# Another order of the pieces in layer 0's rounds, and RWKV mixing and scan as one section with the key-value products in PSUM

## The reference

```
layer 0 (16 heads of 128 columns, D = 256, FF = 1024)
  twice:  h = layer_norm(x);  q = h wq + bq;  k = ctx wk + bk;  v = ctx wv + bv
          one more key and value per head (bias_k, bias_v)
          x = x + softmax(q k / sqrt(128)) v wo + bo
  then:   x = x + gelu(layer_norm(x) w_fc1 + b_fc1) w_fc2 + b_fc2

layer 1 (RWKV, 32 heads of S1 = 8 columns)
  xn = layer_norm(x); sx = xn shifted by one row - xn
  five mixed inputs w, k, v, r, g: xn + sx * (maa + tanh((xn + sx maa_x) w1) w2)
  kT, vT, rT = mixed inputs times Wk, Wv, Wr;  gT = silu(mixed g times Wg)
  wT = exp(-exp(time_decay + tanh(mixed w decay_w1) decay_w2))
  per head: y[t] = r[t] (state[t] + faaaa k[t] v[t]);  state[t+1] = w[t] state[t] + k[t] v[t]
  group norm over each head's 8 columns, times gT, times Wo, added to x
  then channel mixing (a second small section)
layers 2 and 3: two small cross-attentions and a last norm; not touched
```

## Time and profile before

| | |
|---|---|
| median of 3 runs | 1342.48 us (1341.75 to 1343.86) |
| the profiled execution, its own time | 1343.32 us |
| its span, first to last instruction | 1341.6 us |
| what lies around the span | 1.7 us |
| granted TensorE clock, mean | 0.95 |
| layer 0 | 0 to 750 us |
| layer norm of layer 1 | 750 to 761 us |
| mixing | 761 to 832 us |
| scan with all behind it | 832 to 956 us |
| channel mixing | 956 to 986 us |
| layers 2 and 3 | 986 to 1341.6 us |
| busy over the span | PE 88%, PEld 68%, DVE 65%, POOL 48%, ACT 47% |

### The profile page before, as it was taken

The page is one execution under the profiler, slowest core; times in us unless marked ns, Lnnn a source line. Parts: engine busy times, 40 slices in busy tenths (PEclk is TensorE's granted clock), DMA queues, the critical chain, the costliest instruction groups (busy, mean ns, idle before and its releaser), DMA issues. The chain is left out here.

```text
span 1341.6 us, 20628 instructions
## 1 busy us (share of the span) xinstructions
PE 1184.0 (88%) x7388; PEld 907.9 (68%) x7388; DVE 871.7 (65%) x2094; ACT 636.0 (47%) x1425; POOL 647.6 (48%) x673
## 2 busy tenths in 40 slices
PE   6999999999999999999989688766658998899994
PEld 4887888888888788888877533422445775666664
DVE  5776666766667666676665343997555565766666
ACT  3655565555655555655542123002123673477770
POOL 3565665656556565565751031442001672277760
PEclk9999999999999999999999789797799899999997
DMA  5110211101111011210102000000030000000000
GB/s 199 64 48 17 64 64 63 49 17 63 64 64 48 19 61 64 63 48 25 55 17 78 16 1 0 1 0 0 0 88 0 1 2 1 1 1 2 1 2 32
DMA packets 35111, 47.06 MB, mean 35 GB/s; under 512 B 3865, under 2 KB 22082, under 8 KB 35010
## 3 DMA queue, kind: packets, MB, share of 16 engines
q1 hardware_dynamic: 34640, 44.83, 10.4%
q10 hardware_dynamic: 370, 0.91, 0.2%
HBM read 44.69 MB, written 1.05 MB: 34 GB/s over the span
## 5 line engine op out<-in xcount | busy, mean ns | idle before, releaser
L444 POOL TENSOR_TENSOR a_prob<-a_prob,a_inv_total 128x512 f32<-128x512 f32 x128 | 144.1, 1126 | 217.6 <-DVE a_inv_total L732 217.6
L1593 POOL TENSOR_TENSOR l_scores<-l_scores,l_neg_max 128x512 f32<-128x512 f32 x144 | 147.8, 1040 | 99.1 <-DVE l_neg_max L1583 98.8
L1583 DVE CUSTOM_DVE_ANT_0 l_scores<-psum,mask 128x256 f32<-128x256 f32 x384 | 139.8, 421 | 69.6 <-PE psum L1536 69.6
L637 ACT ACTIVATE a_prob<-psum,a_neg_max 128x257 f32<-128x257 f32 x256 | 118.9, 472 | 93.0 <-DVE a_neg_max L729 92.0
L1614 ACT ACTIVATE l_prob_T<-psum 128x512 f32<-128x512 f32 x192 | 108.8, 590 | 34.3 <-PE psum L1550 34.3
L1550 PE MATMUL psum<-ident,l_scores 128*128 128x128 f32 x768 | 116.4, 290 | 7.0 <-POOL l_scores L1593 3.9
L1550 PEld LDWEIGHTS psum<-ident,l_scores 128*128 128x128 f32 x768 | 85.1, 145 | 41.1 <-issue 18.8
L736 DVE TENSOR_TENSOR a_probT_lo<-psum,a_probT_hi 128x512 fp32r<-128x512 f32 x128 | 87.9, 687 | 23.0 <-ACT a_probT_hi L641 22.5
L729 DVE TENSOR_REDUCE a_neg_max<-psum 128x2 f32<-128x514 f32 x128 | 87.3, 682 | 1.3 <-PE psum L486 1.3
L566 PE MATMUL psum<-ident,a_prob 128*128 128x128 f32 x512 | 77.6, 274 | 6.8 <-POOL a_prob_bias L447 6.8
L641 ACT ACTIVATE a_probT_hi<-psum 128x512 fp32r<-128x512 f32 x128 | 76.6, 599 | 9.3 <-PE psum L566 9.3
(11 more groups left out here) (322 smaller groups left out, 3325.4 us busy)
## 6 DMA issues: line engine op xcount, KB each, us to landing
wk_raw<-in_L_xattn_wk SPq DMA_DIRECT2D x16, 512.0 KB, 6.4
wq_raw<-in_L_xattn_wq SPq DMA_DIRECT2D x16, 512.0 KB, 5.7
wv_raw<-in_L_xattn_wv SPq DMA_DIRECT2D x16, 512.0 KB, 3.7
wo_raw<-in_L_xattn_wo SPq DMA_DIRECT2D x16, 512.0 KB, 4.1
ctx_rows<-in_ctx SPq DMA_DIRECT2D x3, 512.0 KB, 4.2
x_rows<-in_x SPq DMA_DIRECT2D x2, 512.0 KB, 9.5
mask<-in_mask_Bx1xSxS_ff SPq DMA_DIRECT2D x1, 1024.0 KB, 8.0
out_dram<-fin_y SPq DMA_DIRECT2D x4, 256.0 KB, 2.1
```

What stands on the lines that cost most here:

```text
L444: pool.tensor_tensor(prob[:, m % 4, :, 0:S], prob[:, m % 4, :, 0:S], rtot[:, m % 4, :].unsqueeze(2).to_broadcast([P, 2, S]), ALU.mult)
L637: act.activation(prob[:, m % 4, q, 0:S + 1], s_bank(g)[:, q, 0:S + 1], ACT.Exp, bias=negm[:, m % 4, q:q + 1], accum_out=tot[:, m % 4, q:q ...
L1583: e = dve.tensor_tensor_reduce(sc[:, i % SC, q, :], s_bank(i)[:, q * S:(q + 1) * S], masks[:, b * NM + q % NM, :], 1.0, BIG, ALU.add, ALU. ...
L1593: pool.tensor_tensor(sc[:, i % SC, :, :], sc[:, i % SC, :, :], m[:, i % SC, :].unsqueeze(2).to_broadcast([P, 2, S]), ALU.subtract).then_in ...
```

## The change

Layer 0: the last pieces of a round change places, S7 before A1, Q3 behind T6, K3 last; the statistics X and the normalising Y become four pieces of one row block each, behind T1 to T4, X in rounds with i % 4 = 0 and Y in those with i % 4 = 1 (POOL's rstd_of moves to the end of the former); L0 and L1 stand behind S0 and S2. A score piece waits for its own head's Q and K alone, and key_columns follows K2 in place of K3.

Layer 1: the two blocks become one, without the barrier. The constants are built at its start, vT's parts during the last mixing, the mixing's products use banks 4 to 7 from pv on, and the first two spreads are issued between mg, pr and pg. The products k v are written back to the PSUM banks that held the spread values; the first state is copied there for each chunk, and the recurrence reads PSUM. POOL's scan_z products wait for one chunk alone. faaaa times k moves to ACT and its product with r to POOL, behind POOL's first scan_z; the product of scan_ru with vT moves from DVE to POOL; the gate (g_T) comes in DVE's order behind the second step. Several tiles share memory. The arithmetic is the same.

```diff
@@ layer0_orders
-    base = ("S0 S1 O0 S2 O1 V0 T0 V1 S3 V2 T1 S4 V3 Q0 T2 S5 Q1 K0 T3 S6 K1 A0 T4 A1 "
-            "S7 T5 Q2 Q3 T6 K2 T7 K3 A2 A3").split()
+    base = ("S0 S1 O0 S2 O1 V0 T0 V1 S3 V2 T1 S4 V3 Q0 T2 S5 Q1 K0 T3 S6 K1 A0 T4 S7 "
+            "A1 T5 Q2 T6 Q3 K2 T7 A2 A3 K3").split()
...
-        if i % NQ == 1:
-            order = put(order, 'V1', 'X0')
-            order = put(order, 'V3', 'X1')
-            order = put(order, 'T3', 'Y0')
-            order = put(order, 'T4', 'Y1')
+        if i % NQ < 2:
+            for t in range(HT):
+                order = put(order, f'T{t + 1}', 'XY'[i % NQ] + str(t))
         if i % NQ == 2:
-            order = put(order, 'V1', 'L0')
-            order = put(order, 'V2', 'L1')
+            order = put(order, 'S0', 'L0')
+            order = put(order, 'S2', 'L1')
@@ stage_layer0, PE, piece S
-                                pe.wait_ge(acc_free, USE[i - 1, 'K3'] + 1)
-                                pe.wait_ge(acc_free, USE[i - 1, 'Q3'] + 1)
                                 pe.wait_ge(kcols, i + 1)
+                            if b == 0:
+                                pe.wait_ge(acc_free, max(USE[i - 1, f'Q{h}'], USE[i - 1, f'K{h}']) + 1)
@@ DVE, piece K
-                                if m == QUAD - 1:
+                                if m == 2:
                                     key_columns(i + 1)
@@ stage_rwkv_mix and stage_rwkv_scan become stage_rwkv; PE
+                def spread_values(e, c):
+
+                    if c == 0:
+                        pe.wait_ge(spread_ok, e + 1)
+                    if e == 0:
+                        pe.wait_ge(v_lo_ok, c + 1)
+                        pe.wait_ge(act_free, nth(num['d2', 1]))
+                    else:
+                        pe.wait_ge(st_ok, (e - 1) * NC + c + 1)
+                    for n in (2 * c, 2 * c + 1):
+                        out = batches(ps[:, n, :])
+                        pe.matmul(out, spread[:, e, :], v_hi[:, c, bh(n), 0:S], start=True, stop=False)
+                        pe.matmul(out, spread[:, e, :], v_lo[:, c, bh(n), 0:S], start=False, stop=True).then_inc(v_full, 1)
+
                 for key in issue:
                     what, n = key
+                    if key == ('pr', 0):
+                        spread_values(0, 0)
+                        spread_values(0, 1)
+                    if key == ('pg', 0):
+                        spread_values(1, 0)
+                    if key == ('pg', 2):
+                        spread_values(1, 1)
...
+                for e in range(2, S1 + LATE):
+                    if e < S1:
+                        for c in range(NC):
+                            spread_values(e, c)
+                    if e == 2:
+                        pe.wait_ge(ruk_ok, NC)
+                        pe.wait_ge(dve_free, nth(num['pg', 3]))
+                        for n in range(4):
+                            pe.matmul(ps[:, 4 + n, :], same[:, :], flat(ruk[:, n // 2, bh(n), :]), start=True, stop=True).then_inc(ru_full, 1)
@@ DVE
+                for e in range(S1):
+                    for c in range(NC):
+                        for n in (2 * c, 2 * c + 1):
+                            dve.wait_ge(v_full, 4 * e + n + 1)
+                            dve.tensor_tensor(batches(ps[:, n, :]), kT[:, c, bh(n), 0:S], batches(ps[:, n, :]), ALU.mult).then_inc(kv_ok, 1)
+                        dve.wait_ge(kv_ok, 4 * e + 2 * c + 2)
+                        dve.tensor_copy(batches(kv_of(c))[:, :, 0:1], m['s0'][:, c, :, e:e + 1]).then_inc(s0_ok, 1)
+                        dve.wait_ge(s0_ok, e * NC + c + 1)
+                        if e >= 2:
+                            dve.wait_ge(z_ok, (e - 2) * NC + c + 1)
+                        dve.tensor_tensor_scan(flat(state[:, e % 2, c, :, :]), flat(wT[:, c, :, :]), kv_of(c), 0.0, ALU.mult, ALU.add).then_inc(st_ok, 1)
+                    if e == 1:
+                        for n in range(4):
...
+                            dve.scalar_tensor_tensor(gT[:, c, half(n)], tanh_of(n), 1.0, ps[:, bank_of(('pg', n)), :], ALU.add, ALU.mult).then_inc(dve_free, 1)
@@ POOL
+                pool.wait_ge(act_free, nth(num['pr', 3]))
+                for e in range(S1):
+                    if e >= 2:
+                        pool.wait_ge(g_full, e - 1)
+                    for c in range(NC):
+                        pool.wait_ge(st_ok, e * NC + c + 1)
+                        pool.tensor_tensor(z[e % 2][:, c, :], rT[:, c, :], flat(state[:, e % 2, c, :, :]), ALU.mult).then_inc(z_ok, 1)
+                    if e == 0:
+                        for c in range(NC):
+                            pool.wait_ge(uk_ok, c + 1)
+                            pool.tensor_tensor(flat(ruk[:, c, :, :]), rT[:, c, :], flat(ruk[:, c, :, :]), ALU.mult).then_inc(ruk_ok, 1)
+                    if e in (3, 4):
+                        c = e - 3
+                        pool.wait_ge(ru_read, 4)
+                        pool.tensor_tensor(batches(att[:, c, :]), batches(ru[:, c, :]), vT[:, c, :, 1:R1], ALU.mult).then_inc(ru_v, 1)
@@ ACT
+                        if what == 'pv' and h == 1:
...
+                            act.activation(v_hi[:, c, :, 0:R1], vT[:, c, :, :], ACT.Copy).then_inc(v_hi_ok, 1)
...
+                        if h == 1:
+                            act.activation(ruk[:, c, :, :], kT[:, c, :, 1:R1], ACT.Identity, scale=chip.vec('L1_xattn_faaaa', c)).then_inc(uk_ok, 1)
```

More of the change, by code:

```diff
@@ L879, in stage_rwkv_mix @@
         mixed = sb("mixed", [P, 3, NC, TOK])
-        dec = sb("dec", [KD, TOK])
         e1 = sb("e1", [P, 2, BANK])
         th = sb("th", [P, 2, BANK])
+        same = sb("same_head", [P, P])
+        dmask = sb("d_mask", [P, S1])
+        spread = sb("spread", [P, S1, P], F32R)
+        gather = sb("gather", [P, S1, P])
+        v_hi, v_lo = sb("v_hi", [P, NC, B, R1 + 1], F32R), sb("v_lo", [P, NC, B, R1 + 1], F32R)
+        state = sb("state", [P, 2, NC, B, S])
+        epsc = sb("eps", [P, 1])
         cur = lambda c: xe[:, c, :, 1:R1]
@@ L911, in begin @@
                 def begin(key):
-                    n = num[key]
-                    if n >= 8:
-                        pe.wait_ge(act_free if uses[n - 8][2] == 'act' else dve_free, nth(n - 8))
-                    return ps[:, n % 8, :]
+                    n, bank = num[key], bank_of(key)
+                    prior = [i for i in range(n) if bank_of(uses[i][:2]) == bank]
+                    if prior:
+                        pe.wait_ge(act_free if uses[prior[-1]][2] == 'act' else dve_free, nth(prior[-1]))
+                    return ps[:, bank, :]
                 def product(key, weight, cols, src, rows=P):
@@ L969, in _ @@
                     for n in range(4):
-                        c, h = ch(n)
-                        dve.wait_ge(full, made['m' + x, n])
-                        dve.scalar_tensor_tensor(batches(scaled[:, i % 2, c, half(n)]), batches(ps[:, num[('m' + x, n)] % 8, :]),
-                                                 chip.vec('L1_xattn_maa_stack', c, MIX[x]), sx[:, c, bh(n), :], ALU.add, ALU.mult).then_inc(dve_free, 1)
+                        if x == 'g' and n % 2 == 0:
+                            values_low(n // 2)
+                        scale(i, x, n)
                     dve.wait_ge(dve_free, nth(num[('m' + x, 3)]))
@@ new lines, in centre @@
+                def centre(i):
+                    n = SEQ[i]
+                    dve.wait_ge(mean_full, i + 1)
+                    dve.scalar_tensor_tensor(att[:, n // 2, half(n)], ps[:, n, :], -1.0 / S1, att[:, n // 2, half(n)], ALU.mult, ALU.add).then_inc(cent_ok, 1)
+                dve.wait_ge(ru_v, NC)
+                for i, n in enumerate(SEQ):
+                    dve.wait_ge(g_full, S1 + i)
+                    dve.tensor_tensor(att[:, n // 2, half(n)], att[:, n // 2, half(n)], ps[:, 4 + n, :], ALU.add).then_inc(att_ok, 1)
+                    if i >= 2:
+                        centre(i - 2)
@@ new lines, in _, with gate @@
+                centre(2)
+                centre(3)
+                def gate(i):
+                    n = SEQ[i]
+                    dve.wait_ge(gn_ok, i + 1)
+                    dve.scalar_tensor_tensor(z[0][:, n // 2, half(n)], att[:, n // 2, half(n)], chip.vec('L1_xattn_gn_b', n // 2), gT[:, n // 2, half(n)],
+                                             ALU.add, ALU.mult).then_inc(gated, 1)
+                for i, n in enumerate(SEQ):
+                    c = n // 2
+                    dve.wait_ge(rstd_ok, i + 1)
+                    dve.scalar_tensor_tensor(att[:, c, half(n)], att[:, c, half(n)], chip.vec('L1_xattn_gn_w', c), sq[:, c, half(n)], ALU.mult, ALU.mult).then_inc(gn_ok, 1)
+                    if i:
+                        gate(i - 1)
@@ L985, in _ @@
+                gate(3)
+                for q in range(4):
+                    dve.wait_ge(o_full, q + 1)
```

(8 more changed lines are left out.)

291 lines of the change are left out of this document (94 added, 197 removed).

## The result

The changed kernel takes 1310.1 us (median; 1306.98 to 1311.75) against 1342.1 for the kernel before (1340.95 to 1343.86): ratio 0.9749, 95% interval 0.9733 to 0.9766, faster. The profiled execution took 1306.98 us, span 1305.2. Forecast were 1301 and a range from 1292 to 1317.

A forecast was written before the change was run, and what follows sets the result against it. It took PE to bound layer 0 and the mixing, and DVE taking turns with POOL the scan. RWKV 32.5 plus layer 0's 9 gave 41.5 us less than 1343.3, 1301.8, or 1301 as median; range 1292 to 1317.

The forecast's parts named there:

- The step: Scan loop: with k v in PSUM the recurrence runs beside POOL's products, 7.4 us a step in place of 9.12.
- The overlap: Mixing to scan: DVE starts step 0 during the mixing, first k v product at 817.8 for 838.57, 20.8 us gained.
- The end of the scan: Behind the last recurrence: one POOL product of 2.35 us, ending at 884.6 for 918.1, 33.5 us less.
- (a): Layer 0, rounds with L: the waits of V2 and Q0 for DVE go, 5.2 us.
- (e): Layer 0, round ends: O0's and A3's waits go with K3 last; 0.67 gained in each of four L rounds, 2.7 us.
- (c): Layer 0's start: the first S no longer waits 1.76 us for the last Q, as it needs Q0 only.
- (b): Layer 0, X and Y spread over eight places: K0's waits of 1.15 and small ones go, 2.7 us.
- The new wait at A3: Layer 0, round ends: A3 waits 0.6 us for T7's lower part; rounds with P before them lose 0.3, three times.
- third rival: Layer 0 gives nothing, the new wait in front of A3 eating the rest: 1310 us, chance 0.14.
- The exclusion stays: Scan: a recurrence or the copy into PSUM still waits for POOL, steps 9.15 to 9.3 us: 1314, chance 0.12.
- PE binds: Scan loop: gathers behind pauses take 6.8 us at half clock, 10.2 a step against 7.4: 1318 us, chance 0.07.
- PSUM slow: Scan loop: DVE reading and writing the same PSUM banks takes twice the time, 55 us: 1356, chance 0.03.

The follow-up runs named there:

- late spreads: The changed kernel with the spreads of k and v for the first two steps behind all of pg: 1325.7 us, ratio 0.9867.
- S7 back: The changed kernel with S7 behind A1 again in layer 0's order, nothing else exchanged: 1297.4 us, ratio 0.9650.
- k v in SBUF: The changed kernel with products k v and the first state written to SBUF tiles, from which the recurrence reads: 1337.6 us, ratio 0.9951.
- K3 between: The changed kernel with S7 behind A1 again and K3 between A2 and A3: 1297.8 us, ratio 0.9653.
- h early: S7 back, with POOL making h's lower half right behind the cut of o's first half, ahead of its normalisations: 1290.7 us, ratio 0.9614.
- RWKV alone: The changed kernel with layer 0's order, statistics, waits and key columns as in the kernel before: 1308.9 us, ratio 0.9738.
- layer 0 alone: The kernel before with only the new order of layer 0, RWKV as it was: 1345.5 us, ratio 1.0015.
- both chunks awaited: The changed kernel with POOL waiting for both chunks' recurrences before a step's first product, as in before: 1316.2 us, ratio 0.9796.

## Why the prediction was right and wrong

The forecast wanted 41.5 us less and the medians give 32.0. In the traces it is 36.4: layer 0 brought 6.3 us too little, RWKV 1.5 more than the 32.5 taken, and 0.3 was lost behind the scan. The other 4.4 lie between the profiled executions and the medians, and no trace shows them. The time lies in the range, but not near the forecast (1294 to 1306 was its neighbourhood, at 0.60): it lies there since the range was drawn to take in the case that layer 0 gives nothing.

In the list below, times of the forecast stand without layer 0's gain, so 2.7 us are added to those of the trace.

- **The step.** 7.4 forecast, 7.42 measured; recurrence 2.29 and products 0.64 each: no surcharge for PSUM as source or target that the times show. The Trainium skill's page SBUF — State Buffer, section Who interferes with whom, lets a DVE instruction with at most one SBUF input run beside GpSimd; the trace agrees (2.29 beside a product of 2.37), and with two SBUF inputs 4.21. The fixed cost of 120 cycles for a PSUM source against 58 for SBUF, which the Trainium skill's page VectorE: DVE Perf Modes, section The TRN2 errata, gives, doesn't show: the recurrence takes 2.29 from PSUM, and 2.29 from SBUF where POOL is idle (873.60 above).
- **The overlap.** First product k v at 817.8 forecast, 818.2 measured. PE through with pg at 834.3, measured 834.7; ruk done 835.5, measured 836.0; gates done 836.8, measured 837.1; end of step 3 at 852.4, measured 853.2, with a wait of 1.29 where 0.6 stood, and 0.78 and 0.56 in step 1 that the sum had not. End of the last recurrence 882.2, measured 883.0. Its worth: 20.8 earlier was to be the start of the first product, and it came 20.4 earlier; in the run with late spreads 13.9 of that is lost, and the rest is the shorter way there (constants and cut of vT moved, no barrier).

```profile
823.79 1.29 DVE L1087 TENSOR_TENSOR psum<-k_T,psum 128x512 f32<-128x512 f32 x2 [0.78 <-PE psum L960]
828.17 1.29 DVE L1087 TENSOR_TENSOR psum<-k_T,psum 128x512 f32<-128x512 f32 x2 [0.56 <-PE psum L960]
843.08 1.29 DVE L1087 TENSOR_TENSOR psum<-k_T,psum 128x512 f32<-128x512 f32 x2 [1.29 <-PE psum L960]
```

- **The end of the scan.** 884.6 forecast, 885.4 measured (POOL's last product, 880.35 and 2.34). From there to channel mixing 37.1 us for 38.4. The 1 us taken back for the clock wasn't needed: it was 1.00 in the loop.

```profile
880.35 2.34 POOL L1158 TENSOR_TENSOR mix_shift<-r_T,mix_state 128x1024 f32<-128x1024 f32 x1 [0.39 <-DVE mix_state L1093]
919.83 0.17 DVE L1240 COPY xn_T<-vecs_T 128x8 f32<-128x8 f32 x1 [3.13 <-PEq L931]
```

- **Layer 0, terms (a), (e) and (c).** Right. The rounds with L are 10.3 us shorter in after, where 5.2 + 2.7 stood. Some 1.7 of it is T7's wait for POOL, forecast to stay at 1.3 and now 0.95 in each of the four. The waits for a_v_lo are gone, and with them the first S's (its row starts 3.4 us earlier, in part by a start that varies: 29.3 to 30.9 in the kernels with the new order).
- **Term (b), X and Y.** The waits of K0 (1.15 and 1.18) are gone, as forecast. Its size can't be read by itself: with S7 back, the rounds with Y are 4.2 us shorter together and those with X 2.6 longer, 1.6 for 2.7, but the other moves act in these rounds too.
- **The new wait at A3.** Forecast 0.6 a round, measured 0.52 to 0.55 in most; 0.27 in three of the rounds with L and 1.05 in the last, where none was expected.
- **The step that failed.** Of the base order the forecast priced Q3, K3 and A3, and passed over S7 in front of A1 in silence. That exchange gives E7 a place in ACT's list ahead of Q2's upper part. With it undone layer 0 ends 16.6 us earlier than before (733.04 for 749.59); less the 1.4 of the clock in round 15 and up to 1.5 of a start that varies, some 14 to 15, so the other terms were together sized rather low at 11.5. With it, 2.7 are left. The third rival (layer 0 gives nothing, 1310) came in its number, but that was luck, since its cause did not: it had the wait in front of A3 eat the gain, and that wait was forecast rightly.
- **The rivals on the scan.** The exclusion stays: fell for this change, and is real in SBUF. PE binds: fell, in the loop no gather takes over 3.7 and the clock is 1.00. Sums and gathers of 5.6 to 5.8 us do come where PE has more pauses, with late spreads and with k v in SBUF. PSUM slow: fell. The forecast reckoned seven steps of turns; in the old kernel it was six.

## What to carry to other kernels

Where an in-order engine's list is reordered, go through the list of every engine that the moved piece feeds, and write down which piece now stands behind which: one piece moved by one place cost some 12 us, most of what the other moves had gained. An operand in PSUM let VectorE work beside GpSimd here, and in this loop that was worth more than a finer grain of waits (27 us against 4, each taken back from the kernel after). Small copies count in it as much as the long instructions: 13.2 us against 12.3.

## What the runs showed of the hardware

- A copy of 4 elements per partition from SBUF to SBUF was stopped by a GpSimd product until that ended (0.61 to 2.08 us, thirteen of sixteen), the same copy to PSUM never (0.17, sixteen times).
- A recurrence with both operands in SBUF and a GpSimd product stopped each other: 4.21 to 4.42 us for 2.29, and 4.36 for 2.35.
- The same piece of TensorE's work behind the same pause of 2.1 us took 5.80 us at a granted clock of 1.00 in one profiled execution and 7.2 in the nine others (0.76 in the four looked at: before, after, K3 between, h early).
- VectorE writing its product back to the PSUM bank that it reads cost the same as writing to SBUF: 1.27 and 1.25 us for two of 512 columns.
- After the scan, the part between the context's layer norm and the last layer norm took 337.7 to 338.3 us in six kernels (before, after, RWKV alone, layer 0 alone, S7 back, K3 between) and 341.0 to 342.3 in the other four, though no edit touches that part. The mean granted clock differs, here in after and with both chunks awaited, 50 us from the same points of the work:

```profile
1001.00:1051.00 50.00, 47.41 (x469) 34.48 (x470) 31.00 (x169) 31.05 (x66) 31.39 (x31) 0.90 0.01 1
1101.00:1151.00 50.00, 46.09 (x258) 30.96 (x257) 36.20 (x137) 25.20 (x46) 17.27 (x16) 0.91 0.00 1
```

```profile
1006.40:1056.40 50.00, 46.81 (x446) 34.16 (x448) 29.99 (x161) 29.82 (x65) 29.71 (x29) 0.86 0.00 1
1106.40:1156.40 50.00, 45.16 (x220) 30.59 (x220) 34.97 (x122) 21.70 (x39) 15.89 (x14) 0.86 0.00 1
```

  0.90 or 0.91 against 0.86 is, as an estimate, some 2 us of work at full speed in 50 us, twice, and so the 4 us. It may be why the profiled execution of after is 3.1 us below its median and that with h early 5.2 above; executions without a record can't show it, so this stays open.
